# Gate rows copied across partitions by DMAs instead of matmuls, and a new order of the layer-1 and layer-2 pairs, in a transformer block with a mixture of experts

## The chip, the cores and the metric

The kernel runs on one core of one Trainium2 chip. The metric is device microseconds for one execution. All tensors are fp32 unless said otherwise.

## The reference

The input `x` is (4 images, 64 channels, 16 x 16 pixels), so 256 tokens per image and 1024 in all. The block is `x = x + attention(ln_c(x))`, followed by a feed-forward part with eight experts, of which each token uses two:

```
logits = xt @ Wr + br;  probs = softmax(logits)
top_p, top_idx = top_k(probs, 2);  weights = top_p / top_p.sum(-1)
xe = xn * ln_g[e] + ln_b[e]
h = gelu(xe @ W1[e] + b1[e])        # 64 -> 256, for each expert e
y = h @ W2[e] + b2[e]               # 256 -> 64
out = sum over the two chosen experts of weights * y
t = t + out
```

## The kernel before, in words

The work is done in two halves of two images (`HALVES`), 512 tokens each (`TOK`). The kernel computes all eight experts for all tokens and multiplies each expert's output by a gate, which is zero for the six experts that a token did not choose. The program of each engine is a list of calls written out by hand; engines wait for each other on semaphores, and nothing on an engine overtakes what stands before it.

**Routing.** `route(h, stage)` on VectorE turns the logits of a half into `gate[h]`, [128 tokens, 4 tiles, 8 experts]. Stages 11 and 12 cut the gate into two fp16 pieces `gcut` (the high part and the rest), 16 columns in a tile of 128. On TensorE `turn_gates(h)` (L894 to L902) turns them by four fp16 matmuls against a fp16 identity, and ScalarE's `turn_gates(h)` (L417) copies the PSUM bank into `gateT[h]`, fp16, [128, 512], in which row e holds expert e's gate for every token.

**Layer 1.** `layer1(q)` (L874) does expert q % 8 of half q / 8: four fp32 matmuls with 256 moving columns, two on the upper and two on the lower 64 rows of the array. ScalarE's `gelu(g)` (L424) follows, two for each `layer1`, into a ring `H` of 16 slots.

**Layer 2.** One step s is a pair of experts of one half (`STEPS` is 8: steps 0 to 3 are half 0, steps 4 to 7 are half 1). `layer2(s)` (L914) is four fp32 matmuls with 512 moving columns; expert 2p fills partitions 0 to 63 of a PSUM bank and expert 2p + 1 fills partitions 64 to 127. Two banks alternate: `layer2(s)` waits until VectorE has read step s - 2.

**Gating.** The gate has to stand on all 64 partitions of its expert. `spread(s)` (L904) does that on TensorE: two fp16 matmuls of a 0/1 selection `sel` against `gateT`. `keep_gates(s)` (L644) on VectorE copies the result into `GS`, and `weigh(s)` (L650) computes (y + b2) * gate. GpSimd's `add_up(s)` (L321) adds the result to the sum of its half, `acc[h]`. `weigh(7)` is done in two pieces of 256 columns.

**End.** `fold_sum` adds the upper and lower 64 partitions of half 0 by matmuls with `fold`. For half 1 `fold_even` takes the first 256 columns of `acc[1]` and of the last step's product; `add_last` on VectorE adds the other 256 columns first, and `fold_odd` folds them. `finish` adds the residual and SyncE's queue sends the result out.

The order of TensorE from `layer1(4)` on is:

```
layer1(4) logits(1) layer1(5) spread(0) layer1(6) layer1(7) turn_gates(1) layer1(8)
layer2(1) spread(1) layer1(9) spread(2) layer1(10) layer2(2) spread(3) layer1(11)
layer2(3) layer1(12) layer2(4) spread(4) layer1(13) spread(5) layer1(14) layer2(5)
layer1(15) layer2(6) spread(6) fold_sum spread(7) layer2(7) fold_even fold_odd
```

SyncE's queue issues the input DMAs in the first ten microseconds and then nothing before the output DMAs.

Of the kernel before, what the change touches and what calls it, by code (L numbers as in the profile page):

```python
# [21 lines left out]
F16 = mybir.dt.float16  # L22
# [21 lines left out]
SG = 2.0 ** 10  # L44
SB = 2.0 ** 8
KG = 2 * E
# [14 lines left out]
def build_block(nc, x, attn_w, ffn_w, w1, w2, b2, out):  # L61
    with ExitStack() as ctx:
# [19 lines left out]
        ps_gates = [banks[:, 5 - 2 * h, :] for h in range(HALVES)]  # L82
        ps_z = [banks[:, k:k + PT, :] for k in (1, 6)]
        ps_y = [banks[:, 4, :], banks[:, 0, :]]
        ps_G = banks[:, 5, :]
# [18 lines left out]
        identh = sb("identh", [P, P], F16)  # L104
        fold = sb("fold", [P, C])
        sel = sb("sel", [P, E, C], F16)
# [45 lines left out]
        gcut = both("gcut", [P, TILES, P], F16)  # L152
        gateT = both("gateT", [P, TOK], F16)
        H = sb("H", [P, RING, TOK])
        GS = both("GS", [P, TOK])
# [23 lines left out]
        identh_ready = sem("identh_ready")  # L179
        fold_ready = sem("fold_ready")  # L180
        sel_step = sem("sel_step")
        sel_ready = sem("sel_ready")
        iota_ready = sem("iota_ready")
        gcut_clear = sem("gcut_clear")
# [47 lines left out]
        gcut_hi = sem("gcut_hi")  # L232
        gcut_ready = sem("gcut_ready")
# [4 lines left out]
        G_ps = sem("G_ps")  # L238
        gs_ready = sem("gs_ready")
        y_ps = sem("y_ps")  # L240
        gated_ready = sem("gated_ready")
# [7 lines left out]
        @block.sync  # L249
        def _(sp):  # L250
            sp.dma_start(X[:, 0:PT, :], x[:, 0:PT, :]).then_inc(x_in[0], 16)
            sp.dma_start(X[:, PT:TILES, :], x[:, PT:TILES, :]).then_inc(x_in[1], 16)
            sp.wait_ge(w_clear, 1)
            for k in range(PT):
                rows = slice(C * k, C * k + C)
                sp.dma_start(WQK[rows, 0, DB * k:DB * k + DB], attn_w[rows, A_WQ:A_WQ + DB]).then_inc(wqk_in, 16)  # L256
            sp.dma_start(X[:, TILES:2 * TILES, :], x[:, TILES:2 * TILES, :]).then_inc(x_in[2], 16)
            for k in range(PT):
                rows = slice(C * k, C * k + C)
                sp.dma_start(WV[rows, k, :], attn_w[rows, A_WV:A_WV + C]).then_inc(wv_in, 16)  # L260
            sp.dma_start(BV[:, :], attn_w[:, A_BV:A_BV + C]).then_inc(bv_in, 16)
            sp.dma_start(W1F[:, 0:2, :, :], w1[:, 0:2, :, :]).then_inc(w1_in[0], 16)
            sp.dma_start(PF[:, :], ffn_w).then_inc(ffn_in, 16)
            for k in range(2):
                sp.dma_start(LB[C * k:C * k + C, :], ffn_w[0:C, F_B:F_B + E]).then_inc(lb_in, 16)
            sp.dma_start(W1F[:, 2:E, :, :], w1[:, 2:E, :, :]).then_inc(w1_in[1], 16)
            for k in range(PT):
                rows = slice(C * k, C * k + C)
                sp.dma_start(WR[rows, k, :], attn_w[rows, A_WR:A_WR + E]).then_inc(wr_in, 16)
            sp.dma_start(W2F[:, :, :], w2).then_inc(w2_in, 16)  # L270
            sp.dma_start(B2F[:, :], b2[0, :, :].rearrange("(p k) c -> p (k c)", k=2)).then_inc(b2_in, 16)
            for n in range(0, TILES, PT):
                sp.wait_ge(res_ready, n // PT + 1)
                sp.dma_start(out[:, n:n + PT, :], res[0][:, n:n + PT, :]).then_inc(out_done, 16)
            for k in range(PT):
                sp.wait_ge(res_ready, IMG + k + 1)
                sp.dma_start(out[:, TILES + k:2 * TILES:PT, :], res[1][:, k:TILES:PT, :]).then_inc(out_done, 16)
            sp.wait_ge(out_done, 16 * 2 * HALVES)

        @block.gpsimd  # L280
        def _(pool):
# [30 lines left out]
            def select_rows():  # L312
                nc.gpsimd.memset(sel[:, :, :], 0.0).then_inc(sel_step, 1)
                for k in range(2):
                    pool.wait_ge(sel_step, k + 1)
                    last = nc.gpsimd.affine_select(out=sel[:, :, :], in_=sel[:, :, :], compare_op=ALU.not_equal,
                                                   fill=1.0 / SG, base=-E * k, pattern=[[-1, E], [0, C]],
                                                   channel_multiplier=1)
                    last.then_inc(sel_step if k == 0 else sel_ready, 1)

            def add_up(s):  # L321

                h, p = s // PAIRS, s % PAIRS
                pool.wait_ge(gated_ready, s + 1)
                if p > 1:
                    pool.wait_ge(acc_ready, (PAIRS - 1) * h + p - 1)
                nc.gpsimd.tensor_tensor(acc[h][:, :], acc[h][:, :], gated[s % 2][:, :], ALU.add)\  # L327
                    .then_inc(acc_ready, 1)
# [7 lines left out]
            for h in range(HALVES):  # L336
                nc.gpsimd.memset(gcut[h][:, :, :], 0.0).then_inc(gcut_clear, 1)
# [3 lines left out]
            nc.gpsimd.tensor_copy(identh[:, :], ident[:, :]).then_inc(identh_ready, 1)  # L341
# [10 lines left out]
            select_rows()  # L352
# [13 lines left out]
        def _(act):  # L366
# [48 lines left out]
            def turn_gates(h):  # L415
                act.wait_ge(gates_ps, h + 1)
                nc.scalar.copy(gateT[h][:, :], ps_gates[h]).then_inc(gateT_ready, 1)  # L417
# [62 lines left out]
        def _(dve):  # L480
# [92 lines left out]
            def route(h, stage):  # L573
# [43 lines left out]
                elif stage == 8:  # L617
                    dve.wait_ge(th_ready, h + 1)
                    for k in range(2):
                        last = nc.vector.tensor_scalar(wab[h][:, k, :], th[h][:, :], (0.5 - k) * SG, 0.5 * SG,  # L620
                                                       ALU.mult, ALU.add)
# [9 lines left out]
                elif stage == 10:  # L631
                    dve.wait_ge(part_ready, h + 1)
                    nc.vector.tensor_tensor(gate[h][:, :, :], part[h][:, 0, :, :], part[h][:, 1, :, :],
                                            ALU.add).then_inc(gate_ready, 1)
                elif stage == 11:
                    dve.wait_ge(gate_ready, h + 1)
                    dve.wait_ge(gcut_clear, h + 1)
                    nc.vector.tensor_copy(gcut[h][:, :, 0:E], gate[h][:, :, :]).then_inc(gcut_hi, 1)
                elif stage == 12:
                    dve.wait_ge(gcut_hi, h + 1)  # L640
                    nc.vector.tensor_tensor(gcut[h][:, :, E:KG], gate[h][:, :, :], gcut[h][:, :, 0:E],
                                            ALU.subtract).then_inc(gcut_ready, 1)

            def keep_gates(s):  # L644
                dve.wait_ge(G_ps, 2 * (s + 1))
                if s > 1:
                    dve.wait_ge(gated_ready, s - 1)
                nc.vector.tensor_copy(GS[s % 2][:, :], ps_G).then_inc(gs_ready, 1)  # L648

            def weigh(s):  # L650
                h, p = s // PAIRS, s % PAIRS
                dve.wait_ge(y_ps, 2 * (s + 1))
                dve.wait_ge(gs_ready, s + 1)
# [8 lines left out]
                for k in range(cuts):  # L662
                    cols = slice(TOK // cuts * k, TOK // cuts * (k + 1))
                    nc.vector.scalar_tensor_tensor(out=dst[:, cols], in0=ps_y[s % 2][:, cols], scalar=B2T[:, p:p + 1],  # L664
                                                   in1=GS[s % 2][:, cols], op0=ALU.add, op1=ALU.mult)\
                        .then_inc(gated_ready, 1)

            def add_last():

                dve.wait_ge(gated_ready, STEPS + 1)  # L670
                dve.wait_ge(acc_ready, 2 * PAIRS - 3)
# [77 lines left out]
            route(0, 11)  # L749
            second_variance(2)  # L750
            route(0, 12)
# [11 lines left out]
            for stage in range(9, 13):  # L763
                route(1, stage)
            keep_gates(0)
            weigh(0)
            keep_gates(1)
            weigh(1)
            keep_gates(2)
            weigh(2)  # L770
            keep_gates(3)
            weigh(3)
            keep_gates(4)
            weigh(4)
            keep_gates(5)
            weigh(5)
            keep_gates(6)
            weigh(6)
            keep_gates(7)
            finish(0)  # L780
# [5 lines left out]
        def _(pe):  # L786
# [107 lines left out]
            def turn_gates(h):  # L894
                pe.wait_ge(identh_ready, 1)
                pe.wait_ge(gcut_ready, h + 1)
                if h == 0:
                    pe.wait_ge(PT_odd, IMG + 1)
                for t in range(TILES):
                    last = nc.tensor.matmul(ps_gates[h][:, P * slot(t):P * slot(t) + P], gcut[h][:, t, :],  # L900
                                            identh[:, :], start=True, stop=True)
                last.then_inc(gates_ps, 1)  # L902

            def spread(s):  # L904
                h, p = s // PAIRS, s % PAIRS
                pe.wait_ge(sel_ready, 1)
                pe.wait_ge(gateT_ready, h + 1)
                if s > 0:
                    pe.wait_ge(gs_ready, s)
                for k in range(2):  # L910
                    nc.tensor.matmul(ps_G[C * k:C * k + C, :], sel[:, 2 * p + k, :], gateT[h][:, :],  # L911
                                     start=True, stop=True).then_inc(G_ps, 1)
# [25 lines left out]
            def fold_sum():  # L938
# [3 lines left out]
                pe.wait_ge(gateT_ready, HALVES)  # L942
# [76 lines left out]
            spread(0)  # L1019
            layer1(6)  # L1020
            layer1(7)
            turn_gates(1)
            layer1(8)
            layer2(1)
            spread(1)
            layer1(9)
            spread(2)
            layer1(10)
            layer2(2)
            spread(3)  # L1030
            layer1(11)
            layer2(3)
            layer1(12)
            layer2(4)
            spread(4)
            layer1(13)
            spread(5)
            layer1(14)
            layer2(5)
            layer1(15)  # L1040
            layer2(6)
            spread(6)
            fold_sum()
            spread(7)
# [60 lines left out]
```

## Time and profile before

| | |
|---|---|
| median of 3 runs | 68.79 us (68.48 to 68.84) |
| profiled execution, its own time | 68.35 us |
| span of the profile | 66.6 us |
| granted TensorE clock | 1.00 throughout, the upper level (2.4 GHz) |
| TensorE busy | 60.2 us, 90% of the span |
| VectorE, ScalarE, GpSimd busy | 38.2, 33.9, 27.6 us |
| matmuls of layer 1 and of layer 2, busy | 18.2 and 15.4 us |

The span runs from the first to the last event that the profile shows; the execution's own time is 1.75 us longer. Busy times of matmuls overlap at their ends, so the distance from one start to the next says what a group costs better than its length does.

### The profile page before, as it was taken

The numbers are of one execution on the slowest core, as the hardware profiler recorded it, in microseconds if no ns is written. First come the engines' busy times: TensorE is split into PE (matmuls) and PEld (weight loads), VectorE is DVE, ScalarE is ACT, GpSimd is POOL, SyncE is SP. The second block draws the span as 40 slices with busy tenths as digits, with TensorE's granted clock in tenths as the row PEclk, the third lists the DMA queues.
The fourth block names the chain that finished last, engine by engine and source line by source line (L and its number), as shares of the span: only waits on it lengthen the run. The fifth ranks groups of instructions, "written<-read, shape, count | busy, mean of one in ns | idle before, by whom it ended". The sixth has DMA issues, their size and how long they took to land.

```text
span 66.6 us, 1224 instructions
## 1 busy us (share of the span) xinstructions
PE 60.2 (90%) x364; PEld 32.9 (49%) x364; DVE 38.2 (57%) x164; ACT 33.9 (51%) x78; POOL 27.6 (41%) x53
## 2 busy tenths in 40 slices
PE   2998799799799999999998799999999999999940
PEld 0315366588356687752765434435152644353630
DVE  2368699279995997931099924807040924049640
ACT  5301356832379995397479991770724392700000
POOL 5766880004599982360798000433443000705200
PEclk9999999999999999999999999999999999999999
DMA  0343478620000000000000000000000000000311
GB/s 0 96 94 57 152 167 253 262 110 5 0 0 0 15 0 0 0 0 0 5 0 0 10 0 0 0 0 0 0 0 0 0 0 0 0 0 0 89 40 43
DMA packets 2959, 2.33 MB, mean 35 GB/s; under 512 B 1924, under 2 KB 2568, under 8 KB 2952
## 3 DMA queue, kind: packets, MB, share of 16 engines
q1 hardware_dynamic: 2632, 2.21, 11.6%
q10 hardware_dynamic: 320, 0.03, 0.4%
q8 instruction: 3, 0.05, 0.3%
q14 instruction: 4, 0.03, 0.2%
HBM read 1.98 MB, written 0.26 MB: 34 GB/s over the span
## 4 chain that ended last, share of the span: by engine, by line
PE 62%; DVE 22%; issue 4%; DMA 4%; SPq 3%; ACT 2%; DVEq 0%
PE banks L927 22%; PE banks L891 21%; PE banks L848 4%; DMA X<-in_x_dram 4%; DVE nmax L519 3%; PE banks L911 3%; PE banks L833 3%; DVE KS L513 2%; DVE X L505 2%; PE banks L870 2%; SPq L256 2%; PE banks L944 2%; ACT PR L388 2%; DVE T L537 1%; DVE X L569 1%
## 5 line engine op out<-in xcount | busy, mean ns | idle before, releaser
L424 ACT ACTIVATE H<-banks,PF 128x512 f32<-128x512 f32 x32 | 20.4, 686 | 11.2 <-PE banks L891 10.8
L891 PE MATMUL banks<-XE,W1F 64*128 64x256 f32 x128 | 18.2, 402 | 0.2 <-ACT H L424 0.2
L927 PE MATMUL banks<-H,W2F 128*64 128x512 f32 x64 | 15.4, 603 | 0.0
L327 POOL TENSOR_TENSOR acc<-acc,gated 128x512 f32<-128x512 f32 x5 | 6.4, 1276 | 19.2 <-DVE gated L664 19.2
L891 PEld LDWEIGHTS banks<-XE,W1F 64*128 64x128 f32 x128 | 11.1, 186 | 6.0 <-issue 4.9
L648 DVE COPY GS<-banks 128x512 f32<-128x512 f32 x8 | 5.5, 685 | 7.1 <-PE banks L911 7.1
L308 POOL TENSOR_SCALAR XE<-XF,PF,LB 128x256 f32<-128x256 f32 x15 | 8.2, 563 | 2.5 <-ACT XF L405 2.5
L789 PE MATMUL banks<-zeros 128*128 128x512 f16 x23 | 8.0, 467 | 1.3 <-POOL zeros L330 1.3
L664 DVE SCALAR_TENSOR_TENSOR gated<-banks,B2T,GS 128x512 f32<-128x512 f32 (+1 forms) x7 | 4.6, 673 | 7.0 <-PE banks L927 6.8
L292 POOL TENSOR_TENSOR rs<-base,half 128x4 f32<-128x4 f32 x4 | 4.1, 1016 | 9.8 <-DVE base L562 9.8
L927 PEld LDWEIGHTS banks<-H,W2F 128*64 128x64 f32 x64 | 4.0, 136 | 6.7 <-issue 6.6
L848 PE MATMUL banks<-V,PTS 128*128 128x64 f32 x32 | 4.3, 277 | 0.1
L848 PEld LDWEIGHTS banks<-V,PTS 128*128 128x128 f32 x32 | 3.9, 191 | 0.9 <-issue 0.9
L789 PEld LDWEIGHTS banks<-zeros 128*128 128x128 f16 x23 | 2.5, 120 | 3.2 <-issue 1.7
L388 ACT ACTIVATE PR<-banks,nmax 128x256 f32<-128x256 f32 x8 | 3.7, 474 | 0.6 <-DVE nmax L519 0.6
L374 ACT ACTIVATE QS<-banks,BQK 64x128 f32<-64x128 f32 x4 | 1.5, 363 | 4.9 <-PE banks L805 4.9
L825 PE MATMUL banks<-KS,QS 32*128 32x256 f32 x16 | 2.8, 421 | 0.4 <-DVE KS L513 0.3
L911 PE MATMUL banks<-gateT,sel 128*64 128x512 f16 x16 | 3.2, 391 | 0.0
L286 POOL TENSOR_TENSOR rs<-base,half 128x2 f32<-128x2 f32 x4 | 2.8, 707 | 0.9 <-DVE base L498 0.9
L519 DVE TENSOR_REDUCE nmax<-banks 128x2 f32<-128x512 f32 x4 | 2.7, 684 | 0.6 <-PE banks L825 0.6
L833 PE MATMUL banks<-ident,PR 128*128 128x128 f32 x16 | 2.5, 280 | 0.4 <-ACT PR L388 0.4
L369 ACT COPY X1T<-banks 128x128 f32<-128x128 f32 x4 | 1.0, 261 | 3.4 <-PE banks L796 3.4
(87 smaller groups left out, 71.9 us busy)
## 6 DMA issues: line engine op xcount, KB each, us to landing
W1F<-in_w_dram SPq DMA_DIRECT2D x1, 768.0 KB, 6.0
W2F<-in_w_dram SPq DMA_DIRECT2D x1, 512.0 KB, 5.5
W1F<-in_w_dram SPq DMA_DIRECT2D x1, 256.0 KB, 3.2
out_dram<-res SPq DMA_DIRECT2D x4, 64.0 KB, 1.8
X<-in_x_dram SPq DMA_DIRECT2D x2, 64.0 KB, 1.9
X<-in_x_dram SPq DMA_DIRECT2D x1, 128.0 KB, 2.4
WQK<-in_attn_w_dram ACTq DMA_DIRECT2D x2, 16.0 KB, 2.1
WQK<-in_attn_w_dram SPq DMA_DIRECT2D x2, 8.0 KB, 2.0
```

The source lines that it names most:

```text
L308: nc.gpsimd.tensor_scalar(XE[h][:, e, :], XF[h][:, :, :].rearrange("p i n -> p (i n)"), PF[:, F_G + e:F_G + e + 1], LB[:, e:e + 1], ALU.mu ...
L327: nc.gpsimd.tensor_tensor(acc[h][:, :], acc[h][:, :], gated[s % 2][:, :], ALU.add)\
L388: last = nc.scalar.activation(PR[h][:, k, :], ps_S[i % 2][:, t, :], ACT.Exp, bias=nmax[h][:, k:k + 1], accum_out=total[h][:, k:k + 1])
L424: nc.scalar.activation(H[:, r, :].rearrange("p (t n) -> p t n", t=PT), ps_z[g // J % 2][:, :, PIX * j:PIX * j + PIX], ACT.Gelu, bias=PF[:, ...
L519: nc.vector.tensor_reduce(nmax[i // IMG][:, im], ps_S[i % 2], AX_X, ALU.max, negate=True)\
L648: nc.vector.tensor_copy(GS[s % 2][:, :], ps_G).then_inc(gs_ready, 1)
L664: nc.vector.scalar_tensor_tensor(out=dst[:, cols], in0=ps_y[s % 2][:, cols], scalar=B2T[:, p:p + 1], in1=GS[s % 2][:, cols], op0=ALU.add, ...
L789: nc.tensor.matmul(banks[:, bank, :], zeros[:, 0:P], zeros[:, :], start=True, stop=True)
L848: last = nc.tensor.matmul(ps_O[:, t, :], PTS[i // IMG][:, i % IMG, m, P * t:P * t + P], V[i // IMG][:, n + m, :], start=(m == 0), stop=(m ...
L891: nc.tensor.matmul(ps_z[q % 2][:, k, PIX * j:PIX * j + PIX], W1F[rows, e, j, :], XE[h][rows, e, :], start=True, stop=True).then_inc(z_read ...
L911: nc.tensor.matmul(ps_G[C * k:C * k + C, :], sel[:, 2 * p + k, :], gateT[h][:, :], start=True, stop=True).then_inc(G_ps, 1)
L927: mm = nc.tensor.matmul(ps_y[s % 2][C * k:C * k + C, :], W2F[:, u, :], H[:, (2 * J * s + J * k + j) % RING, :], start=(j == 0), stop=(j == ...
```

## The change

The gate is no longer cut into fp16 pieces: stages 11 and 12, the `gcut`, `identh` and `sel` tiles and what fills them are gone. `turn_gates(h)` turns the fp32 gate itself, with its eight columns as the stationary operand and the fp32 identity moving; `gateT[h]` is fp32, [8, 512], and both halves use PSUM bank 5. `spread` and `keep_gates` are gone. In their place SyncE's queue issues two DMAs for each step, 16 in all: each reads one row of `gateT[h]` (512 fp32, one partition) and writes it to 64 partitions of a tile `GS[s]` of its own. `weigh(s)` waits for both. `layer2(1)` moves ahead of `layer1(6)`, and from then on pairs of `layer1` alternate with one `layer2`; `fold_sum` comes before `layer2(6)`. `finish(0)` moves ahead of `weigh(6)` on VectorE, and `add_up(6)` on GpSimd is done in two pieces.

```
@@ SyncE, behind the input DMAs and ahead of the output DMAs
+            for s in range(STEPS):
+                h, p = s // PAIRS, s % PAIRS
+                if p == 0:
+                    sp.wait_ge(gateT_ready, h + 1)
+                for k in range(2):
+                    sp.dma_start(GS[s][C * k:C * k + C, :],
+                                 gateT[h][2 * p + k:2 * p + k + 1, :].unsqueeze(1).broadcast_to([1, C, TOK])).then_inc(gates_in[s], 16)
@@ GpSimd
-            select_rows()
-            nc.gpsimd.tensor_copy(identh[:, :], ident[:, :]).then_inc(identh_ready, 1)
-                nc.gpsimd.memset(gcut[h][:, :, :], 0.0).then_inc(gcut_clear, 1)
@@ add_up
-                nc.gpsimd.tensor_tensor(acc[h][:, :], acc[h][:, :], gated[s % 2][:, :], ALU.add)\
-                    .then_inc(acc_ready, 1)
+                cuts = 2 if s == STEPS - 2 else 1
+                for k in range(cuts):
+                    cols = slice(TOK // cuts * k, TOK // cuts * (k + 1))
+                    nc.gpsimd.tensor_tensor(acc[h][:, cols], acc[h][:, cols], gated[s % 2][:, cols], ALU.add)\
+                        .then_inc(acc_ready, 1)
@@ VectorE, weigh
-                dve.wait_ge(gs_ready, s + 1)
+                dve.wait_ge(gates_in[s], 32)
@@ add_last
-                dve.wait_ge(acc_ready, 2 * PAIRS - 3)
+                dve.wait_ge(acc_ready, 2 * PAIRS - 2)
@@ TensorE, turn_gates
-                pe.wait_ge(gcut_ready, h + 1)
+                pe.wait_ge(gate_ready, h + 1)
+                else:
+                    pe.wait_ge(gateT_ready, h)
-                    last = nc.tensor.matmul(ps_gates[h][:, P * slot(t):P * slot(t) + P], gcut[h][:, t, :],
-                                            identh[:, :], start=True, stop=True)
+                    last = nc.tensor.matmul(ps_gates[:, P * slot(t):P * slot(t) + P], gate[h][:, t, :], ident[:, :],
+                                            start=True, stop=True)
@@ fold_sum
-                pe.wait_ge(gateT_ready, HALVES)
+                pe.wait_ge(scaled_ready, HALVES)
```

TensorE's order after the change, from `layer1(4)` on:

```
layer1(4) logits(1) layer1(5) layer2(1) layer1(6) layer1(7) turn_gates(1) layer2(2)
layer1(8) layer1(9) layer2(3) layer1(10) layer1(11) layer2(4) layer1(12) layer1(13)
layer2(5) layer1(14) layer1(15) fold_sum layer2(6) layer2(7) fold_even fold_odd
```

## Rows read from the trace of the kernel before

**Rows 1.** The page: busy time and share of the span, by engine.

```profile
PE 60.2 (90%) x364; PEld 32.9 (49%) x364; DVE 38.2 (57%) x164; ACT 33.9 (51%) x78; POOL 27.6 (41%) x53
```

**Rows 2.** Windows: stretch, length, busy by engine, clock, DMA share, GB/s.

```profile
22.00:33.00 11.00, 11.00 (x78) 7.09 (x77) 6.40 (x48) 7.97 (x17) 5.73 (x9) 1.00 0.01 1
...
37.30:62.10 24.80, 24.78 (x147) 11.05 (x148) 10.60 (x17) 11.56 (x19) 6.38 (x5) 1.00 0.00 1
```

**Rows 3.** TensorE's timeline, 27 to 49 us: start, length, instructions, idle before.

```profile
27.65 0.40 PE L900 MATMUL banks<-identh,gcut 128*128 128x128 f16 x4
27.98 1.13 PE L891 MATMUL banks<-XE,W1F 64*128 64x256 f32 x8
...
34.11 0.41 PE L911 MATMUL banks<-gateT,sel 128*64 128x512 f16 x2
34.45 1.14 PE L891 MATMUL banks<-XE,W1F 64*128 64x256 f32 x8
35.76 1.14 PE L891 MATMUL banks<-XE,W1F 64*128 64x256 f32 x8 [0.17 <-ACT H L424]
37.32 0.38 PE L900 MATMUL banks<-identh,gcut 128*128 128x128 f16 x4 [0.43 <-DVE gcut L641]
37.64 1.13 PE L891 MATMUL banks<-XE,W1F 64*128 64x256 f32 x8
38.70 1.94 PE L927 MATMUL banks<-H,W2F 128*64 128x512 f32 x8
40.47 0.39 PE L911 MATMUL banks<-gateT,sel 128*64 128x512 f16 x2
40.78 1.14 PE L891 MATMUL banks<-XE,W1F 64*128 64x256 f32 x8
...
46.40 1.94 PE L927 MATMUL banks<-H,W2F 128*64 128x512 f32 x8
48.27 1.14 PE L891 MATMUL banks<-XE,W1F 64*128 64x256 f32 x8
```

**Rows 4.** TensorE's timeline at the end, 58 to 62 us.

```profile
58.58 0.39 PE L911 MATMUL banks<-gateT,sel 128*64 128x512 f16 x2
58.89 1.10 PE L944 MATMUL banks<-fold,acc 128*128 128x64 f32 x8
59.93 0.41 PE L911 MATMUL banks<-gateT,sel 128*64 128x512 f16 x2
60.17 1.88 PE L927 MATMUL banks<-H,W2F 128*64 128x512 f32 x8
```

**Rows 5.** VectorE's timeline: end of the second routing, and the last gating.

```profile
36.55 0.19 DVE L633 TENSOR_TENSOR gate<-part 128x32 f32<-128x32 f32 x1
...
52.34 0.75 DVE L664 SCALAR_TENSOR_TENSOR acc<-banks,B2T,GS 128x512 f32<-128x512 f32 x1
...
62.13 0.88 DVE L664 SCALAR_TENSOR_TENSOR gated<-banks,B2T,GS 128x256 f32<-128x256 f32 x2 [0.57 <-PE banks L927]
```

**Rows 6.** TensorE's timeline: two fp32 matmuls with 128 moving columns, and the next start.

```profile
13.71 0.66 PE L805 MATMUL banks<-X1T,WQK 128*128 128x128 f32 x4
14.21 0.27 PE L796 MATMUL banks<-ident,X 128*128 128x128 f32 x1
```

**Rows 7.** ScalarE's and GpSimd's timelines: the turned gates' copy, two gelus; a bias add.

```profile
28.09 0.59 ACT L417 CAST gateT<-banks 128x512 f16<-128x512 f32 x1 [1.13 <-PE banks L900]
...
29.87 1.30 ACT L424 ACTIVATE H<-banks,PF 128x512 f32<-128x512 f32 x2
```

```profile
6.98 0.72 POOL L300 TENSOR_TENSOR XV<-X,BV 128x256 f32<-128x256 f32 x1 [0.88 <-DMA BV<-in_attn_w_dram]
```

**Rows 8.** DMA issues: size and median us to landing; and the queue's timeline.

```profile
X<-in_x_dram SPq DMA_DIRECT2D x1, 128.0 KB, 2.4
...
3.47 1.25 SPq L260 DMA_DIRECT2D WV<-in_attn_w_dram  x2
```

**Rows 9.** Windows of half a microsecond while the weights load (columns as in rows 2).

```profile
12.50:13.00 0.50, 0.50 (x6) 0.50 (x7) 0.02 (x1) 0.26 (x2) 0.00 (x0) 1.00 0.81 328
```

More of the change, by code:

```diff
@@ L43 @@
 EPS_C, EPS_T = 1e-6, 1e-5
-SG = 2.0 ** 10
-SB = 2.0 ** 8
-KG = 2 * E
 WARM = 8
@@ L81, in build_block @@
         ps_L = [banks[:, 3 * h, 0:TILES * E] for h in range(HALVES)]
-        ps_gates = [banks[:, 5 - 2 * h, :] for h in range(HALVES)]
+        ps_gates = banks[0:E, 5, :]
         ps_z = [banks[:, k:k + PT, :] for k in (1, 6)]
         ps_y = [banks[:, 4, :], banks[:, 0, :]]
-        ps_G = banks[:, 5, :]
         ps_b2 = banks[:, 3, 0:PAIRS]
@@ L103, in build_block @@
         ident = sb("ident", [P, P])
-        identh = sb("identh", [P, P], F16)
         fold = sb("fold", [P, C])
-        sel = sb("sel", [P, E, C], F16)
         zeros = sb("zeros", [P, TOK], F16)
@@ L151, in build_block @@
         gate = both("gate", [P, TILES, E])
-        gcut = both("gcut", [P, TILES, P], F16)
-        gateT = both("gateT", [P, TOK], F16)
+        gateT = both("gateT", [E, TOK])
         H = sb("H", [P, RING, TOK])
-        GS = both("GS", [P, TOK])
+        GS = [sb(f"GS{s}", [P, TOK]) for s in range(STEPS)]
         gated = both("gated", [P, TOK])
@@ L178, in build_block @@
         ident_ready = sem("ident_ready")
-        identh_ready = sem("identh_ready")
         fold_ready = sem("fold_ready")
-        sel_step = sem("sel_step")
-        sel_ready = sem("sel_ready")
         iota_ready = sem("iota_ready")
-        gcut_clear = sem("gcut_clear")
         b2_ps = sem("b2_ps")
@@ L231, in build_block @@
         gate_ready = sem("gate_ready")
-        gcut_hi = sem("gcut_hi")
-        gcut_ready = sem("gcut_ready")
         gates_ps = sem("gates_ps")
@@ L237, in build_block @@
         h_ready = sem("h_ready")
-        G_ps = sem("G_ps")
-        gs_ready = sem("gs_ready")
         y_ps = sem("y_ps")
+        gates_in = [sem(f"gates_in{s}") for s in range(STEPS)]
         gated_ready = sem("gated_ready")
@@ L310, in stretch @@
                                         ALU.mult, ALU.add).then_inc(xe_ready, 1)
[L312 to L319, printed above, removed]
             def add_up(s):
@@ L335, in _ @@
                                     base=0, pattern=[[-1, P]], channel_multiplier=1).then_inc(ident_ready, 1)
-            for h in range(HALVES):
-                nc.gpsimd.memset(gcut[h][:, :, :], 0.0).then_inc(gcut_clear, 1)
             first_pow(0)
@@ L416, in turn_gates @@
                 act.wait_ge(gates_ps, h + 1)
-                nc.scalar.copy(gateT[h][:, :], ps_gates[h]).then_inc(gateT_ready, 1)
+                nc.scalar.copy(gateT[h][:, :], ps_gates).then_inc(gateT_ready, 1)
             def gelu(g):
@@ L619, in route @@
                     for k in range(2):
-                        last = nc.vector.tensor_scalar(wab[h][:, k, :], th[h][:, :], (0.5 - k) * SG, 0.5 * SG,
+                        last = nc.vector.tensor_scalar(wab[h][:, k, :], th[h][:, :], 0.5 - k, 0.5,
                                                        ALU.mult, ALU.add)
@@ L634, in route @@
                                             ALU.add).then_inc(gate_ready, 1)
[L635 to L648, printed above, removed]
             def weigh(s):
@@ L664, in weigh @@
                     nc.vector.scalar_tensor_tensor(out=dst[:, cols], in0=ps_y[s % 2][:, cols], scalar=B2T[:, p:p + 1],
-                                                   in1=GS[s % 2][:, cols], op0=ALU.add, op1=ALU.mult)\
+                                                   in1=GS[s][:, cols], op0=ALU.add, op1=ALU.mult)\
                         .then_inc(gated_ready, 1)
@@ L748, in _ @@
             second_moments(2)
-            route(0, 11)
             second_variance(2)
-            route(0, 12)
             sum_tokens(3)
@@ L762, in _ @@
             route(1, 7)
-            for stage in range(9, 13):
-                route(1, stage)
-            keep_gates(0)
+            route(1, 9)
+            route(1, 10)
             weigh(0)
-            keep_gates(1)
             weigh(1)
-            keep_gates(2)
             weigh(2)
-            keep_gates(3)
             weigh(3)
-            keep_gates(4)
             weigh(4)
-            keep_gates(5)
             weigh(5)
-            keep_gates(6)
+            finish(0)
             weigh(6)
-            keep_gates(7)
-            finish(0)
             weigh(7)
@@ L894, in turn_gates @@
             def turn_gates(h):
-                pe.wait_ge(identh_ready, 1)
-                pe.wait_ge(gcut_ready, h + 1)
+                pe.wait_ge(gate_ready, h + 1)
                 if h == 0:
                     pe.wait_ge(PT_odd, IMG + 1)
+                else:
+                    pe.wait_ge(gateT_ready, h)
                 for t in range(TILES):
-                    last = nc.tensor.matmul(ps_gates[h][:, P * slot(t):P * slot(t) + P], gcut[h][:, t, :],
-                                            identh[:, :], start=True, stop=True)
+                    last = nc.tensor.matmul(ps_gates[:, P * slot(t):P * slot(t) + P], gate[h][:, t, :], ident[:, :],
+                                            start=True, stop=True)
                 last.then_inc(gates_ps, 1)
[L904 to L912, printed above, removed]
             def layer2(s):
@@ L1018, in _ @@
             layer1(5)
-            spread(0)
+            layer2(1)
             layer1(6)
@@ L1022, in _ @@
             turn_gates(1)
+            layer2(2)
             layer1(8)
-            layer2(1)
-            spread(1)
             layer1(9)
-            spread(2)
+            layer2(3)
             layer1(10)
-            layer2(2)
-            spread(3)
             layer1(11)
-            layer2(3)
+            layer2(4)
             layer1(12)
-            layer2(4)
-            spread(4)
             layer1(13)
-            spread(5)
+            layer2(5)
             layer1(14)
-            layer2(5)
             layer1(15)
+            fold_sum()
             layer2(6)
-            spread(6)
-            fold_sum()
-            spread(7)
             layer2(7)
```

## The prediction, made before the change was run

> **What bounds the kernel now.** I read the busy shares first: TensorE is busy 90% of the span, no other engine over 57% [rows 1]. A share over the whole span can mislead, so I then asked for windows. From 22 to 33 us TensorE is busy all of the time, and from 37.3 to 62.1 us it is busy 24.78 of 24.80 us, while VectorE has 10.6 and ScalarE 11.6 us of work there, and the DMA engines are idle [rows 2]. The reader is to see that in these stretches only TensorE's own list counts. Between them lies the one hole: in TensorE's timeline `layer1(6)` starts at 34.45 and costs 1.06 (38.70 - 37.64, a pair of starts further on), so `layer1(7)` could start at 35.51 and starts at 35.76; it would end at 36.82, and `turn_gates(1)` starts at 37.32, released by the last cut of the gate [rows 3]. That is 0.25 + 0.50 = 0.75 us of waiting. Behind the last `layer2` stands a tail of 66.6 - 62.1 = 4.5 us of gating, folding, residual and output.
>
> So I price each edit by TensorE's starts, and then ask whether the new source of the gates comes in time.
>
> **Spread matmuls.** There are eight. Behind a `layer1` one costs 34.45 - 34.11 = 0.34 us [rows 3]. Behind a `layer2` it takes 40.78 - 40.47 = 0.31, but that `layer2` costs 40.47 - 38.70 = 1.77 where one followed by a `layer1` costs 48.27 - 46.40 = 1.87 [rows 3], so 0.21 net. The one ahead of `layer2(7)` takes 60.17 - 59.93 = 0.24 [rows 4]. Three stand behind a `layer1` (0, 2, 5), four behind a `layer2` (1, 3, 4, 6): 3 x 0.34 + 4 x 0.21 + 0.24 = 2.10 us, all on TensorE's path. Gain 2.10.
>
> **The hole at 37 us.** `layer2(1)` now stands ahead of `layer1(6)` and fills 1.87 us while VectorE routes half 1; its inputs were ready before (gelus 6 and 7 end at 29.87 + 1.30 = 31.17 [rows 7]). Stages 11 and 12 are gone too, so `turn_gates(1)` needs only `gate`, written at 36.55 + 0.19 = 36.74 [rows 5], or about 37.4 with the delay of the next part. TensorE comes to it at about 38.7. `layer1(7)` finds its gelus done for the same reason. Gain 0.75, and nothing on that engine has to wait instead.
>
> **Turning fp32 gates.** Before, `turn_gates` costs 27.98 - 27.65 = 0.33 us [rows 3]. Afterwards it is four fp32 matmuls with 128 moving columns. No row has eight stationary columns. From below: `layer2` moves 2 x 512 columns in 1.77 us, 1.73 ns each, so 4 x 128 columns take 0.89. From above: two fp32 matmuls with 128 moving and 128 stationary columns take 14.21 - 13.71 = 0.50 [rows 6], so four take 1.0, or 1.1 by the loosest of its four places (0.55). Narrow weights are nearer to the lower end; I take 0.95, a loss of 0.62 each, 1.24 for two. Both lie on the path: rows 2 show TensorE full around the first, and the second no longer stands in a hole. Range of the two together: 1.12 to 1.54.
>
> **VectorE and GpSimd.** Eight copies of 0.68 us, two cuts, a memset and two selections vanish. These engines have spare time in these stretches [rows 2], so I cost this at nothing. It only matters where they set the end, which is the next part.
>
> **The end.** `layer2(7)` now follows `layer2(6)` directly. `weigh(6)` takes 0.75 [rows 5] and `add_up(6)` two pieces at 0.72 each by the 256-column add [rows 7]. With `layer2(6)` ending 1.8 to 1.9 us before `layer2(7)`, the first piece is there at +1.5 us and the second at +2.2. `fold_even` needs the first at about +1.9, `add_last` needs the second only behind both halves of `weigh(7)`, at +1.9 + 0.9 = +2.8 [rows 5]. Both fit, by 0.4 and 0.6 us. `finish(0)`, 0.5 us, is done before `weigh(6)`, because `fold_sum` ends 1.8 us earlier. So the tail stays 4.5 us. Without that cover it would grow by a few tenths.
>
> **Order.** No `layer1` waits on a gelu: two gelus take 1.3 us [rows 7], and a pair of `layer1` plus a `layer2` takes 2 x 1.06 + 1.87 = 4.0 us for four gelus (2.6 us). `layer2(7)` needs the gelus of `layer1(15)`, which end about 1.6 us after it; `fold_sum` and `layer2(6)` give 2.8.
>
> **Sum.** -2.10 - 0.75 + 1.24 = -1.61 us. `layer2(7)` ends at about 60.5 instead of 62.1, the span is 65.0, the profiled time 68.35 - 1.6 = 66.75. The profiled execution lies 0.44 below the median of the runs, so against those the forecast is 68.79 - 1.6 = 67.2 us, -2.3%.
>
> **The transfers, on which all of this hangs.** `gateT[0]` is copied at 28.09 to 28.68 [rows 7], with the longer turn until about 29.3. A DMA issue takes about 0.6 us (two in 1.25) [rows 8], 1.2 for a step, so eight take 5 us. A load of 128 KB lands after 2.4 us [rows 8], of which the bytes take 0.4 at the 328 GB/s of rows 9, so about 2.0 us are fixed. From about 31.3 us on, 16 x 131,072 bytes = 2.10 MB have to be written. When are they needed? Step 0 at 37.4, where VectorE is free; step 3 at the end of `layer2(3)`, about 45.6; step 7 at 60.4. The last asks for 2.10 MB in 29.1 us, 72 GB/s; step 3 asks for 1.05 MB in 14.3, 73 GB/s. SyncE's queue holds only the output DMAs behind these, and `weigh` is what waits. The trace shows loads at 328 GB/s over half a microsecond [rows 9]. At that rate, 4.5 times what is needed, the transfers cost nothing.
>
> No row shows what they really are: 64 packets of 2 KB read from one and the same partition. The other bound is that reads of one partition go one behind the other, as if one DMA engine did them. One engine moves 328 / (16 x 0.81) = 25.3 GB/s [rows 9]. Then one DMA takes 5.2 us, a step 10.4, all 16 take 82.9 us. The loads in the trace are spread over 128 partitions, so they don't tell the two apart. I take the transfers as hidden, since a rate 4.5 times below the one seen would still do, by a chance little better than even.
>
> The trace shows 328 GB/s with all 128 partitions as destination. The Trainium skill (SBUF, section on the DMA port swizzle) says that the rate depends on how many of 16 ports the partitions reach, that eight partitions share a port, and that four partitions alone reach about 27 GB/s. The source here is one partition, so by that rule a DMA takes 4.8 us and the kernel would come out at about 115 us; no run here shows it yet.
>
> **Rivals.**
> (a) *One partition feeds all reads at about one engine's rate.* VectorE waits in `weigh(s)` for DMA after DMA, the banks of `layer2` stay full, and TensorE waits. The last gates land at 31.3 + 82.9 = 114.2 us, with the tail of 4.5 the span is 118.7 and the time 68.79 + 52.1 = 120.9 us. For it: a single source, and nothing in the trace that refutes it. Against it: no row shows a limit of this kind either, and the queue otherwise idles. It decides as soon as the rate falls under about 70 GB/s. The skill's port rule, cited above, is this rival with its own figure.
> (b) *The same, at a middle rate*, say twice one engine's, 50.6 GB/s: 41.4 us, the last gates at 72.7, the span 77.2, time 68.79 + 10.6 = 79.4 us.
> (c) *The turns and the tail eat the gain.* Turns at 1.54, a tail longer by 0.4, and the spreads worth only the 0.21 everywhere (1.68): -1.68 - 0.75 + 1.54 + 0.4 = -0.5, 68.3 us, hardly to be told from no change. Rows of starts speak against it.
> (d) *The transfers keep up at the start but lag at the end*, at 68 to 72 GB/s: within 0.3 us of before, 68.8.
>
> **How the numbers follow.** About 0.5% (0.35 us) is what a measurement of this kernel can tell from no change. Forecast 0.48; (a) 0.35; (b) 0.10; (c) and (d) together 0.07, of which 0.05 within 0.5%, 0.01 on either side. Faster 0.49, same 0.05, slower 0.46. The likeliest case alone goes from 66.4 (all eight spreads at 0.34, turns at 1.12: -2.72 - 0.75 + 1.12 = -2.35) to 67.9 (turns at 1.54 and the tail 0.4 longer: -0.91). With rival (a) so likely the range must reach it: 66.4 to 121.
>
> **What would show it.** Right: no matmuls between the `layer1` and `layer2` groups, TensorE without idle time from 22 to about 60.4 us, `turn_gates` at 0.9 to 1.0 us, a landing time of the gate DMAs below 6 us, VectorE's `weigh` released by TensorE. Wrong: `weigh` released by a DMA, steps spaced by 10 us (5 in rival (b)), and TensorE idle for most of the second half. The forecast is wrong in size, not in kind, if `turn_gates` costs over 1.1 us, if a gelu holds a `layer1`, or if GpSimd's add releases `fold_even`.

## The result, and the profile after

The changed kernel takes 106.15 us (median of 4 runs, 105.96 to 106.48) against 68.81 us before: a ratio of 1.544, 95% interval 1.537 to 1.551. It is slower by half. The forecast was 67.2 us. The stated range (66.4 to 121) holds the time only because rival (a) stood in it.

The page first, the busy line as in [rows 1] and the slices of the clock and the DMA:

```profile
span 104.4 us, 1189 instructions
...
PE 67.7 (65%) x356; PEld 36.8 (35%) x356; DVE 32.6 (31%) x152; ACT 33.3 (32%) x78; POOL 24.6 (24%) x48
...
PEclk9999999999999999769999955799975557855555
DMA  1436800000029889888989987788998699889502
GB/s 42 82 103 197 298 37 3 0 9 0 0 12 29 26 27 29 25 36 38 38 27 28 27 31 33 57 27 27 28 27 27 59 30 28 25 25 35 64 5 50
```

TensorE is no longer the bound: 65% instead of 90%. From the 13th slice to the 37th the 16 DMA engines are busy for 80% of the time or more in nearly every slice and move 25 to 38 GB/s (57 and 59 in two slices), where the weights earlier came at 298. So it is not that one engine does all the work: nearly all of them are occupied, and little gets through. What they wait for is the question of the experiments.

The chain that ended last (start, length, what) is SyncE's queue issuing one gate DMA after another:

```profile
28.89 0.58 ACT gateT L402
29.49 0.51 SPq L264
29.99 0.04 issue
30.04 0.60 SPq L264
30.63 0.04 issue
30.68 1.95 SPq L264
32.62 0.04 issue
32.67 4.76 SPq L264
37.43 0.04 issue
37.47 4.78 SPq L264
...
47.10 4.13 SPq L264
...
65.70 2.94 SPq L264
...
78.32 3.91 SPq L264
82.23 0.04 issue
82.27 2.07 SPq L264
...
84.38 14.95 DMA GS<-gateT
```

Two issues take 0.5 to 0.6 us, as in [rows 8], the third 1.95. From the fourth on SyncE gets rid of one only as fast as the DMAs ahead of it are done: mostly 4.77 us for 131,072 bytes, 27.5 GB/s, with the four shorter ones shown (4.13, 2.94, 3.91, 2.07). The median time from issue to landing is 15.5 us, where a load of the same size took 2.4 [rows 8].

VectorE's timeline shows who waits; these answer to [rows 5]:

```profile
37.32 0.19 DVE L618 TENSOR_TENSOR gate<-part 128x32 f32<-128x32 f32 x1
41.35 0.75 DVE L634 SCALAR_TENSOR_TENSOR acc<-banks,B2T,GS 128x512 f32<-128x512 f32 x1 [3.83 <-DMA GS<-gateT]
50.31 0.75 DVE L634 SCALAR_TENSOR_TENSOR gated<-banks,B2T,GS 128x512 f32<-128x512 f32 x1 [8.21 <-DMA GS<-gateT]
59.98 0.75 DVE L634 SCALAR_TENSOR_TENSOR gated<-banks,B2T,GS 128x512 f32<-128x512 f32 x1 [8.92 <-DMA GS<-gateT]
67.48 0.75 DVE L634 SCALAR_TENSOR_TENSOR gated<-banks,B2T,GS 128x512 f32<-128x512 f32 x1 [6.75 <-DMA GS<-gateT]
...
93.09 0.75 DVE L634 SCALAR_TENSOR_TENSOR gated<-banks,B2T,GS 128x512 f32<-128x512 f32 x1 [8.79 <-issue]
99.42 0.88 DVE L634 SCALAR_TENSOR_TENSOR gated<-banks,B2T,GS 128x256 f32<-128x256 f32 x2 [5.57 <-DMA GS<-gateT]
```

Seven of the eight steps are released by a DMA; for step 6 (at 93.09) the view names no releaser, but its wait of 8.79 us looks like the others. The steps are 6 to 10 us apart. TensorE's timeline, to be read beside [rows 3]:

```profile
27.81 1.04 PE L861 MATMUL banks<-ident,gate 128*8 128x128 f32 x8
28.78 1.13 PE L851 MATMUL banks<-XE,W1F 64*128 64x256 f32 x8
...
60.83 3.68 PE L878 MATMUL banks<-H,W2F 128*64 128x512 f32 x8 [5.81 <-issue]
```

A turn costs 28.78 - 27.81 = 0.97 us. In some stretches behind long waits the granted clock is at the lower level (1.2 GHz, the 5s in the slices): the `layer2` at 60.83, behind 5.81 us of idle time, takes 3.68 us where it took 1.94. It mostly costs nothing here, since TensorE is waiting anyway; from `weigh(7)` on to the end of the span it is 104.4 - 99.4 = 5.0 us against 4.5 before.

### The profile page after: what moved, and what is told of

It is laid out like the page before. It is cut to its first block, busy times and chain, and to the rows that moved or that the text cites. A ratio compares the mean times of both kernels' runs of the same rounds, so it can differ in the third digit from the quotient of the medians.

```text
span 104.4 us, 1189 instructions
## 1 busy us (share of the span) xinstructions
PE 67.7 (65%) x356; PEld 36.8 (35%) x356; DVE 32.6 (31%) x152; ACT 33.3 (32%) x78; POOL 24.6 (24%) x48
## 4 chain that ended last, share of the span: by engine, by line
SPq 54%; DMA 17%; PE 13%; DVE 10%; issue 2%; ACT 2%; DVEq 0%
SPq L264 52%; DMA GS<-gateT 14%; PE banks L851 3%; PE banks L808 3%; DMA X<-in_x_dram 2%; DVE nmax L504 2%; PE banks L793 2%; DVE KS L498 1%; DVE X L490 1%; SPq L242 1%; PE banks L908 1%; ACT PR L373 1%; PE banks L861 1%; DVE T L522 1%; DVE X L554 1%
## 5 line engine op out<-in xcount | busy, mean ns | idle before, releaser
L878 PE MATMUL banks<-H,W2F 128*64 128x512 f32 x64 | 21.7, 811 | 19.6 <-issue 19.6
L409 ACT ACTIVATE H<-banks,PF 128x512 f32<-128x512 f32 x32 | 19.8, 682 | 26.6 <-PE banks L851 26.6
L316 POOL TENSOR_TENSOR acc<-acc,gated 128x512 f32<-128x512 f32 (+1 forms) x6 | 6.5, 1084 | 51.7 <-DVE gated L634 51.7
L878 PEld LDWEIGHTS banks<-H,W2F 128*64 128x64 f32 x64 | 5.4, 169 | 29.6 <-issue 29.5
L851 PEld LDWEIGHTS banks<-XE,W1F 64*128 64x128 f32 x128 | 12.6, 206 | 7.7 <-issue 6.0
L904 PE MATMUL banks<-fold,acc 128*128 128x64 f32 x4 | 1.1, 435 | 7.2 <-POOL acc L316 7.2
L634 DVE SCALAR_TENSOR_TENSOR acc<-banks,B2T,GS 128x512 f32<-128x512 f32 x2 | 1.5, 751 | 13.0 <-DMA GS<-gateT 13.0
L904 PEld LDWEIGHTS banks<-fold,acc 128*128 128x128 f32 x4 | 0.9, 322 | 8.7 <-POOL acc L316 8.7
L908 PE MATMUL banks<-fold,gated 128*128 128x64 f32 x4 | 1.1, 435 | 4.1 <-DVE gated L634 4.1
## 6 DMA issues: line engine op xcount, KB each, us to landing
GS<-gateT SPq DMA_DIRECT2D x16, 128.0 KB, 15.5
```

Source lines behind the costliest of these rows:

```text
L316: nc.gpsimd.tensor_tensor(acc[h][:, cols], acc[h][:, cols], gated[s % 2][:, cols], ALU.add)\
L409: nc.scalar.activation(H[:, r, :].rearrange("p (t n) -> p t n", t=PT), ps_z[g // J % 2][:, :, PIX * j:PIX * j + PIX], ACT.Gelu, bias=PF[:, ...
L851: nc.tensor.matmul(ps_z[q % 2][:, k, PIX * j:PIX * j + PIX], W1F[rows, e, j, :], XE[h][rows, e, :], start=True, stop=True).then_inc(z_read ...
L878: mm = nc.tensor.matmul(ps_y[s % 2][C * k:C * k + C, :], W2F[:, u, :], H[:, (2 * J * s + J * k + j) % RING, :], start=(j == 0), stop=(j == ...
```

## The experiments

Eight kernels were run; each is compared with runs of the kernel before on the same chip (medians 68.40 to 68.46 us). A number in brackets is the 95% interval of the ratio.

**1. No gate DMAs.** How much of the loss are the transfers, and what are the other edits worth?

```
-            for s in range(STEPS): ... sp.dma_start(GS[s] ...)
-                dve.wait_ge(gates_in[s], 32)
+                if s == 0:
+                    dve.wait_ge(w1_in[1], 16)
-                                                   in1=GS[s][:, cols]
+                                                   in1=W1F[:, 2:4, :, :].rearrange("p e j m -> p (e j m)")[:, cols]
```

> Leaves out the gating itself: no gate DMAs are issued, and the weighing reads a constant slice of the layer-1 weights in place of the gate rows, with no wait for a DMA. Everything else of the changed kernel stays. Theory (the transfers are the whole loss, the other edits gain what the sum said): 67.2 us, 1.6 below before, TensorE full from 22 to 60.4 us, turns near 0.95 us each. Rival (the new order, the fp32 turns or the tail also cost): 68.3 us or more.

Measured: 65.69 us, 0.959 (0.955 to 0.963). The transfers are more than the whole loss, and the other edits gain 2.76 us, not the 1.6 of the sum. TensorE's timeline shows where the rest comes from:

```profile
33.68 1.13 PE L845 MATMUL banks<-XE,W1F 64*128 64x256 f32 x8
34.74 1.94 PE L872 MATMUL banks<-H,W2F 128*64 128x512 f32 x8
36.61 2.00 PE L845 MATMUL banks<-XE,W1F 64*128 64x256 f32 x16
38.54 1.04 PE L855 MATMUL banks<-ident,gate 128*8 128x128 f32 x8
39.51 1.94 PE L872 MATMUL banks<-H,W2F 128*64 128x512 f32 x8
```

One `layer1` alone costs 34.74 - 33.68 = 1.06 us, two in a row cost 38.54 - 36.61 = 1.93, which is 0.19 less than twice 1.06. There are five such pairs: 0.95 us that the sum did not have.

**2. The same DMAs from 64 partitions.** Same queue, bytes, destinations, waits; only the source is wide.

```
-                                 gateT[h][2 * p + k:2 * p + k + 1, :].unsqueeze(1).broadcast_to([1, C, TOK])
+                                 W1F[C * k:C * k + C, 2 * p:2 * p + 2, :, :].rearrange("p e j m -> p (e j m)")
```

> Same 16 DMAs, same queue, same destinations, bytes and waits, but each reads 64 different partitions of the layer-1 weights (512 fp32 of each) in place of one gate row 64 times; so the gating is by wrong numbers. Theory (reads of one source partition are served at about 27 GB/s): the source no longer limits, a DMA takes 0.6 to 1.2 us, all land before they are needed, 67.2 us as without DMAs, within 0.3. Rival 1 (any copy within SBUF to 64 partitions in 2 KB packets is this slow, or the destination limits): still 4.8 us for a DMA and about 106 us. Rival 2 (SyncE's queue): issues of 4.8 us remain, about 106 us.

Measured: 65.75 us, 0.960 (0.956 to 0.964). The DMA issues of this kernel, with their size and median time to landing, and a window (columns as in [rows 2]) while the DMAs of the first half run:

```profile
GS<-W1F SPq DMA_DIRECT2D x16, 128.0 KB, 2.3
```

```profile
31.50:35.50 4.00, 4.00 (x27) 2.38 (x27) 1.58 (x16) 2.39 (x6) 2.87 (x6) 1.00 0.93 205
```

2.3 us instead of 15.5, and 205 GB/s instead of 27.5. This excludes SyncE's queue, the destination of 64 partitions and the copy within SBUF as causes. What is left is the source: one partition, read 64 times. The 205 GB/s are no measure of what the wide source could give: no issue is held up here, each takes 0.60 us (at most 0.603) with a gap of 0.04 to the next, and 131,072 bytes in 0.64 us are just 205 GB/s. The Trainium skill (SBUF — State Buffer, section on the DMA port swizzle) says that 64 partitions reach eight of the 16 ports, about 218 GB/s. The 205 lie below that, but since the issues alone explain them, no run here tests it.

**3. Gate rows four partitions apart.** Rows at 0, 4, 8 to 28 instead of 0 to 7.

```
-        ps_gates = banks[0:E, 5, :]
+        ps_gates = banks[0:4 * E, 5, :]
-        gate = both("gate", [P, TILES, E])
+        gate = both("gate", [P, TILES, 4 * E])        # zeros between
-                                 gateT[h][2 * p + k:2 * p + k + 1, :]
+                                 gateT[h][4 * (2 * p + k):4 * (2 * p + k) + 1, :]
```

> Same computation; the turned gate rows stand 4 partitions apart (0, 4, 8 to 28) in place of 0 to 7, by a stationary operand of 32 columns with zeros between. Each DMA still reads one partition. Theory, strict form (a group of neighbouring partitions shares one way out, and DMAs in the queue overlap where their source groups differ, as the four shorter steps of the changed kernel suggest): two or more DMAs in flight run side by side, so 69.9 us from first issue to last landing shrinks to 35 to 50 and the time is 71 to 86 us. Rival (the limit is on a single DMA or a single partition and they run one after another whatever the rows): 16 x 4.8 us stay, 104 to 113 us.

Measured: 73.30 and 74.73 us in two runs, against 68.45 before; the trace is that of the first. The transfers took from the first issue at 29.57 to the last weighing at 66.58, 37 us instead of 70:

```profile
66.58 0.88 DVE L638 SCALAR_TENSOR_TENSOR gated<-banks,B2T,GS 128x256 f32<-128x256 f32 x2 [3.31 <-DMA GS<-gateT]
```

With 2.0 us fixed that is 2.10 MB in 35 us, 60 GB/s. That is the rate of about two DMAs side by side, though eight source rows lie in eight groups; what holds it there was not tried. It is still under the 72 GB/s that the prediction named, and the kernel is still slower than before.

**4. Half the bytes.** `gateT` and `GS[s]` in fp16, one rounding of the gate.

```
-        gateT = both("gateT", [E, TOK])
+        gateT = both("gateT", [E, TOK], F16)
-        GS = [sb(f"GS{s}", [P, TOK]) for s in range(STEPS)]
+        GS = [sb(f"GS{s}", [P, TOK], F16) for s in range(STEPS)]
```

> Gate rows and their spread copies are fp16 (one rounding of the gate), so each of the 16 x 64 packets has 1 KB in place of 2 KB. Theory (a rate in bytes): 2.4 us for a DMA, 35 us for all, time about 72 us (106 - 34). Rival (a price for each packet read from the same partition, 4.8 us / 64 = 75 ns): no change, 106 us.

Measured: 70.11 us, 1.023 (1.018 to 1.029). The issues last up to 2.41 us, half of 4.78, though there are as many packets as before. It is a rate in bytes, not a price of a packet.

**5. Rows 32 partitions apart.** Is it the distance that matters, or which group a partition is in?

```
-        gate = both("gate", [P, TILES, E])
+        gate = both("gate", [P, TILES, 2, 32])        # expert 2p + k in column 32k + p
-                                 gateT[h][2 * p + k:2 * p + k + 1, :]
+                                 gateT[h][32 * k + p:32 * k + p + 1, :]
```

> As the changed kernel, but the turned gate rows of a pair of experts stand 32 partitions apart: 0 and 32, 1 and 33, 2 and 34, 3 and 35 (a stationary operand of 64 columns). Theory 1 (partitions 0 to 3 and 32 to 35 share one way out, as the Trainium skill's page SBUF, section on the DMA port swizzle, has it): no two DMAs can run side by side, 16 x 4.77 = 76.3 us in a row, last gates at about 108 us, 114 to 115 us in all, slower than the changed kernel. Theory 2 (only a distance of four partitions or more matters): like the rows 4 apart, about 74 us.

Measured: 115.16 us, 1.682 (1.677 to 1.688), at the upper end of the 114 to 115 of theory 1. VectorE's timeline shows even steps:

```profile
41.69 0.75 DVE L639 SCALAR_TENSOR_TENSOR acc<-banks,B2T,GS 128x512 f32<-128x512 f32 x1 [3.85 <-DMA GS<-gateT]
51.35 0.75 DVE L639 SCALAR_TENSOR_TENSOR gated<-banks,B2T,GS 128x512 f32<-128x512 f32 x1 [8.91 <-DMA GS<-gateT]
60.96 0.75 DVE L639 SCALAR_TENSOR_TENSOR gated<-banks,B2T,GS 128x512 f32<-128x512 f32 x1 [8.86 <-DMA GS<-gateT]
70.60 0.75 DVE L639 SCALAR_TENSOR_TENSOR gated<-banks,B2T,GS 128x512 f32<-128x512 f32 x1 [8.88 <-DMA GS<-gateT]
```

A step takes 9.6 to 9.8 us, twice 4.8, and only the last is a little shorter (9.0); of SyncE's issues from the fourth on none is under 4.76 us. From the first issue (29.82) to the last weighing (108.62) it is 78.8 us, and 16 x 4.77 + 2.0 is 78.3. Partitions 0 to 3 and 32 to 35 do share one way out. The Trainium skill's partition table (SBUF — State Buffer, section on the DMA port swizzle) has them on one port, and this trace agrees. The limit belongs to the group and not to a row that is read again and again: here each pair of DMAs reads two different partitions and gains nothing, while in experiment 3 single rows in different groups did overlap. The changed kernel used partitions 0 to 3 and 4 to 7, two groups; this accounts for its four shorter issues and for the 9 us by which it ended sooner than this one.

**6. Through HBM.** The turned gates go to a scratch tensor in HBM, and the 16 DMAs read the rows there.

```
                 if p == 0:
                     sp.wait_ge(gateT_ready, h + 1)
+                    sp.dma_start(rows_dram[h, :, :], gateT[h][:, :]).then_inc(rows_out, 16)
+                    sp.wait_ge(rows_out, 16 * (h + 1))
-                                 gateT[h][2 * p + k:2 * p + k + 1, :].unsqueeze(1).broadcast_to([1, C, TOK])
+                                 rows_dram[h, 2 * p + k:2 * p + k + 1, :].broadcast_to([C, TOK])
```

> Same computation; each half's turned gates go out to a scratch tensor in HBM by one DMA of 16 KB, and the 16 spreading DMAs read the rows there. Theory (only the SBUF source partition limits): about 2 us more before the first spreading DMA, which then lands at about 36 us, later ones 1.2 us a step; weighing of step 0 starts at 37.5 to 38 us, nothing waits on a DMA after it: 67.2 to 67.6 us, faster than both kernels. Rival (reads of one 2 KB row by all DMA engines are slow from HBM too): over 80 us.

Measured: 65.81 us, 0.962 (0.960 to 0.965): the whole computation, faster than both kernels. The queue's timeline, and a window from `layer1(2)` to near the end of `layer2(7)`:

```profile
29.45 0.28 SPq L265 DMA_DIRECT2D gate_rows<-gateT  x1
30.91 4.94 SPq L268 DMA_DIRECT2D GS<-gate_rows  x8
```

```profile
26.70:59.50 32.80, 32.80 (x208) 17.11 (x207) 11.18 (x46) 18.92 (x34) 11.84 (x16) 1.00 0.21 70
```

The detour costs 1.5 us up to the first spreading issue, eight issues take 4.9 us, and TensorE is busy 32.80 of 32.80 us. Reading one row 64 times is no trouble by itself, from HBM.

**7. Sixteen source rows.** VectorE writes the gate 16 times, so that each turned row stands on 16 partitions, 8 apart, and a DMA reads each of them four times.

```
-        gate = both("gate", [P, TILES, E])
+        gate = both("gate", [P, TILES, P // E, E])
-                                 gateT[h][2 * p + k:2 * p + k + 1, :].unsqueeze(1).broadcast_to([1, C, TOK])
+                                 gateT[h][2 * p + k:P:E, :].unsqueeze(1).broadcast_to([P // E, C * E // P, TOK])
```

> Same computation; the gate is written 16 times by VectorE (stationary operand of 128 columns), so that every gate row stands on 16 partitions, 8 apart, after the turn, and each DMA reads 16 partitions four times each. Still 16 DMAs of 128 KB. Theory (rate grows with the number of source partition groups, 8 of them here): a DMA takes 0.6 to 1.0 us, all hidden; VectorE's wide gate costs about 0.4 us more a half, hidden before the second turn: 67.2 to 67.7 us. Rival (it is the repeated reading, not the single partition): four reads of a row still run one after another on its partition group and it stays over 80 us.

Measured: 66.04 us, 0.965 (0.962 to 0.968), landing after 2.4 us. The same 16 DMAs within SBUF, with their repeated reads, are hidden once their source spans enough groups. The wide gate takes VectorE 0.69 us instead of 0.19, to 38.18, but the second turn does not wait for it:

```profile
36.92 2.00 PE L852 MATMUL banks<-XE,W1F 64*128 64x256 f32 x16
38.85 1.16 PE L862 MATMUL banks<-ident,gate 128*128 128x128 f32 x8
39.94 1.94 PE L879 MATMUL banks<-H,W2F 128*64 128x512 f32 x8
```

It starts 1.93 us after the pair of `layer1` does, as in experiment 1, so nothing holds it up. What it costs is more: 39.94 - 38.85 = 1.09 us with 128 stationary columns, against 0.97 with eight. Two turns make 0.24 us, about the difference between this kernel and that of experiment 6.

**8. The order alone**, on the kernel before, with its spread matmuls and copies. The start of TensorE's list of calls, before and after:

```
-layer1(5) spread(0) layer1(6) layer1(7) turn_gates(1) layer1(8) layer2(1) spread(1) layer1(9) spread(2) ...
+layer1(5) layer2(1) spread(0) layer1(6) layer1(7) turn_gates(1) spread(1) layer2(2) spread(2) layer1(8) layer1(9) ...
```

> The kernel before, with its fp16 turns, spread matmuls and copies, and only the new order: layer2(1) ahead of layer1(6), layer1 in adjacent pairs, fold_sum ahead of layer2(6), finish(0) ahead of weigh(6). The spreads stand beside a layer2 or fold_sum, never inside a pair. Theory (two adjacent layer1 cost 1.93 us, not 2 x 1.06; the hole of 0.75 closes): -0.75 - 5 x 0.19 = -1.7, about 66.8 us. Rival (the pairs are cheaper only because nothing else runs there, or the closed hole reopens at a spread): 67.7 us or more.

Measured: 66.54 us, 0.973 (0.970 to 0.976). So 1.86 of the 2.65 us of experiment 6 come from the order and 0.79 from the exchange of spreads for DMAs. The intervals leave about 0.3 us either way on the 0.79. The prediction's own terms for that exchange, with the turn as measured, give 2.10 - 2 x (0.97 - 0.33) = 0.82. But 2.10 was worked out for the spreads' old places. At their new ones seven of them cost 1.69 us (from `layer2(1)` to `fold_sum` it is 20.98 us here and 19.94 in experiment 6, whose turn is 0.65 longer) and the last about 0.2, so 1.9, which makes the exchange 0.6. The measurement can't tell the two apart.

GpSimd's `add_up(6)` is still in one piece here, and `fold_even` waits for it:

```profile
60.26 0.66 PE L953 MATMUL banks<-fold,acc 128*128 128x64 f32 x4 [0.29 <-POOL acc L327]
```

The tail from `weigh(7)` on is nonetheless 64.5 - 60.04 = 4.46 us, as long as before.

## Why the prediction was wrong, point by point

**The step that failed** is "I take the transfers as hidden". It was a choice between two bounds, 328 GB/s and 25.3 GB/s, and the lower one was nearly right: 27.5 GB/s by the issues, 30.9 over the whole (2.10 MB in 69.85 us from first issue to last landing, less 2.0). Experiments 1 and 2 show that this and nothing else made the kernel slower; 3, 5 and 7 show that the rate rises with the number of source groups, and 4 that it is a rate in bytes. The prediction worked out 115 us from the Trainium skill's figure for four partitions (SBUF — State Buffer, section on the DMA port swizzle); the changed kernel needs 9 less because its rows lie in two groups, and with all rows in one group it is 115.16. A rate of 4.5 times less than the one seen looked like ample room, but the rate seen had 128 partitions at its end and this one had one: the nearest row in bytes was not the nearest in shape.

**Rival (a)** named the picture of the profile, steps about 10 us apart, released by DMAs, TensorE idle, and the mechanism in the main: a narrow source feeds all reads. But its unit is a group of partitions, not one partition, and its "as if one DMA engine did them" is not what happens, since the 16 engines together are mostly over 80% busy. That one engine's rate (25.3 GB/s) came so close to one group's (27.5) is luck as far as the runs show. It gave 120.9 us; the term that was mis-sized is the 82.9 us for 16 DMAs, measured 67.9: 6.6 less by the rate (16 x 4.77 = 76.3) and 8.4 by the overlap of the two groups.

**Spread matmuls and turns.** The turn is right: 0.95 forecast, 0.97 measured, and 1.09 with wide weights in experiment 7, so narrow weights do cost less, by 0.12. The 2.10 for the spreads fits experiment 8 against 6 (0.79 against 0.82) but is not shown by it, since the places differ.

**The hole.** Right: in experiment 6 TensorE has no idle time from 26.7 to 59.5 us, the second turn included.

**The end and GpSimd.** Right in the time: in experiment 1 the tail from `weigh(7)` is 63.9 - 59.45 = 4.45 us, as before (66.6 - 62.13 = 4.47). The two pieces of `add_up(6)` were not needed for it: experiment 8 has one and a tail of 4.46.

**The order.** Too small: the prediction priced `layer1` at 1.06 wherever it stood and missed 5 x 0.19 = 0.95 us. With it the sum is -2.56, and -2.76 was measured in experiment 1. The remaining 0.2 is within the interval of that measurement (2.5 to 3.1 us); why a pair is cheaper was not tried.

**The chances.** 0.46 stood on slower. With a worked figure at hand that spoke for rival (a) and no row against it, there was no ground for holding "faster" the likeliest.

## What to carry to other kernels

Before SBUF rows are spread by DMA, count the partitions that the source spans, not the bytes or the idle queue: one partition fed all 16 DMA engines at 27.5 GB/s here. With the rows written to HBM first, or turned onto 16 partitions 8 apart, the same spreading was hidden behind TensorE (65.81 and 66.04 us). Price a group of matmuls by its neighbours as well as by its kind: two adjacent `layer1`, whose matmuls use half the array's rows, were 0.19 us cheaper than two apart.

## What the runs showed of the hardware that was not expected

DMAs in one queue that read different source groups run side by side, but with eight groups at hand the rate was only that of about two (60 GB/s, against 27.5). A queue that is behind shows as long issues: mostly 4.77 us each instead of 0.6, so the 16 issues held SyncE itself for 59.67 us. And where nothing holds the DMAs up, the issues set the pace: DMAs of 128 KB, one every 0.64 us, moved 205 GB/s (experiment 2).
